# A two-layer kernel: layer 1's weights quantised during the experts, its products and recurrence turned to tokens on partitions

## The reference, cut to what matters

```python
u = rmsnorm(xn, norm_w)                       # per token
a = exp(-sigmoid(dt) * |A|)
x_t = a * x_(t-1) + sigmoid(dt) * (u @ Bmat)  # 64 states, over the 1024 tokens of a batch
s = x_t @ C + D                               # (tokens, 128)
def fp4(v):   # blocks of 16 along the last axis, scale = max|block| / 6, values on the grid 0..6
def lin(x, w): return fp4(x) @ fp4(w).T
f = lin(silu(lin(xn, w_gate)) * lin(xn, w_up), w_down)    # inner width 352
x = x + s * silu(f)
```

## Time and profile before

| what | us |
|---|---|
| timed runs, median of 3 | 1974.12 |
| timed runs, lowest and highest | 1966.82, 1975.07 |
| the profiled execution's own time | 1962.93 |
| its span, first to last instruction | 1960.8 |
| PE busy / DVE / ACT / POOL | 1828.6 / 1506.1 / 1012.8 / 1424.2 |
| mean granted TensorE clock | 0.971 |

### The profile page before, as it was taken

One profiled execution on the slowest core, in us unless ns is written; L12 is line 12 of the kernel. 1 busy time (PEld: TensorE's weight loads), 2 busy tenths in 40 slices (PEclk: granted clock), 3 DMA queues, 4 the chain that ended last, 5 costly groups with the idle time before them and its releaser, 6 DMA issues. The chain is left out here.

```text
span 1960.8 us, 33201 instructions
## 1 busy us (share of the span) xinstructions
PE 1828.6 (93%) x10425; PEld 1045.9 (53%) x10425; DVE 1506.1 (77%) x2045; ACT 1012.8 (52%) x1513; POOL 1424.2 (73%) x862
## 2 busy tenths in 40 slices
PE   6899999999999999999999999999998799965776
PEld 5455555555555555555555555555554688753345
DVE  5877777777777777777777777777777688787776
ACT  4345544454454455444544544554544588754543
POOL 3388888888888888888888888888887166636453
PEclk9899999999999999999999999999999799986899
DMA  6101010110101010101101010101010677230000
GB/s 219 45 12 55 19 54 21 43 46 19 54 11 54 11 55 19 54 21 43 45 21 54 11 54 11 55 19 54 21 43 21 216 246 243 79 92 19 0 17 27
DMA packets 98115, 107.82 MB, mean 55 GB/s; under 512 B 8224, under 2 KB 88032, under 8 KB 94880
## 3 DMA queue, kind: packets, MB, share of 16 engines
q1 hardware_dynamic: 93088, 97.15, 15.1%
q0 software_dynamic: 4992, 10.27, 1.5%
HBM read 52.56 MB, written 26.82 MB: 40 GB/s over the span
## 5 line engine op out<-in xcount | busy, mean ns | idle before, releaser
L1154 POOL TENSOR_TENSOR psum_k<-psum_k,probs 128x1024 f32<-128x1024 f32 x384 | 925.5, 2410 | 199.2 <-ACT probs L1099 184.2
L1171 DVE TENSOR_REDUCE mxh<-ps_m 128x2 f32<-128x1024 f32 x518 | 633.5, 1223 | 255.0 <-PE ps_m L931 253.4
L1099 ACT ACTIVATE probs<-ps_s 128x1024 f32<-128x1024 f32 x512 | 497.4, 1023 | 264.0 <-PE ps_s L948 212.8
L956 PE MATMUL ps_v<-probs,V 128*64 128x512 f32 x2056 | 489.8, 597 | 0.0
L1195 DVE RECIPROCAL rden<-den 128x128 f32<-128x128 f32 x260 | 245.6, 946 | 25.2 <-ACT den L1068 16.0
L956 PEld LDWEIGHTS ps_v<-probs,V 128*64 128x64 f32 x2056 | 137.2, 137 | 235.9 <-issue 233.4
L931 PE MATMUL ps_m<-k_hi,q_hi 64*128 64x512 f32 x1036 | 237.8, 452 | 11.1 <-DVE mxh L1171 7.2
L946 PE MATMUL ps_s<-q_lo,k_hi 64*128 64x512 f32 x1024 | 202.8, 389 | 0.0
L948 PE MATMUL ps_s<-shift,ones_r 64*128 64x512 f32 x1024 | 202.7, 388 | 0.0
L946 PE MATMUL ps_s<-q_hi,k_lo 64*128 64x512 f32 x1024 | 202.2, 389 | 0.0
L946 PE MATMUL ps_s<-q_hi,k_hi 64*128 64x512 f32 x1024 | 202.0, 390 | 0.0
(11 more groups left out here) (317 smaller groups left out, 2840.7 us busy)
## 6 DMA issues: line engine op xcount, KB each, us to landing
e_ew<-w_split SPq DMA_DIRECT2D x23, 1024.0 KB, 7.3
V<-V_next SPq DMA_DIRECT2D x33, 512.0 KB, 3.3
xs_hi<-xh SPq DMA_DIRECT2D x16, 512.0 KB, 3.7
xs_lo<-xl SPq DMA_DIRECT2D x16, 512.0 KB, 4.3
rows<-in_blank_d SPq DMA_DIRECT2D x4, 1483.5 KB, 18.6
e_x_raw<-rows SPq DMA_DIRECT2D x23, 258.0 KB, 3.5
we_raw<-in_experts_d SPq DMA_DIRECT2D x33, 128.0 KB, 2.4
w_split<-we_hi SPq DMA_DIRECT2D x32, 128.0 KB, 1.8
```

What stands on the lines that cost most here:

```text
L956: ins = nc.tensor.matmul(ps_v[rows, :], V[par][:, kt, rows], probs[:, t % RING, x, :], start=kt == 0, stop=kt == KT - 1)
L1099: nc.scalar.activation(probs[:, t % RING, :, :], ps_s[t % 2][:, :, :], ACT.Exp, scale=SCALE).then_inc(p_done, 1)
L1154: nc.gpsimd.tensor_tensor(acc, probs[:, (t - 1) % RING, :, :] if kt == 1 else acc, probs[:, t % RING, :, :], ALU.add).then_inc(add_done, 1)
L1171: nc.vector.tensor_reduce(mxh[:, kh, t, :], max_bank(unit, i)[:, :, :], AX.X, ALU.max).then_inc(m_done, 1)
```

## The change

In the experts:

- The shared weights are loaded after those of tiles 2 and 3, with layer 1's weights behind them; ACT splits the shared weights in tile 1 and DVE in tile 2.
- DVE runs steps 0 to 3 of the quantisation of layer 1's gate and up weights (128x768) and down weights (128x352) in blocks 9 to 12, ACT takes their sizes in tile 3, and POOL does the rest (four operations each, all in float32) ahead of its first scatter. They lie in the space of the `e_y` buffers, so `sums(0)` now also waits for PE's transposes of them, which stand in tiles 23 to 25.
- The transposes of the attention output go into the shared tiles 27 to 30 and the tail (`attended`), with ACT's silu four tiles after a chunk's own tile, and DVE's product (`gated`) behind it. The tail of PE has four `attended` ahead of the last `token_rows`; the tail of DVE has `gated(4)` between `weighted(5)` and `weighted(6)`, and so on.
- Half of X (batches 0 and 1) is loaded into the `y_row` buffers behind `sums(1)`.

In layer 1:

- No weights, no attention transposes and no X of batches 0 and 1 are loaded or formed at the start. The order is input, gate and up products, then states. Chunk 0 and chunk 1 are quantised one after the other, and `moments(3)` stands behind `hidden(0, 3)`.
- The down product has the transposed h stationary (12 products of 128 columns for three of 512), the recurrence the states stationary, with D added by a product of ones and a row (8 products of 128 columns). Both give tokens on partitions. `token_rows` and ACT's `finish` go; POOL adds x1 (`finish`) at the head of its stream for the chunk.
- One recurrence a chunk, behind its down product, in place of two groups of four.
- ACT takes the sizes of B and of the input ahead of `normalise`, `hidden_T` and `input_T` in chunks 0, 1 and 3.

The diff, cut to its core:

```diff
@@ expert_tiles, sync @@
-            sp.dma_start(ws_raw[:, :], g.inp["shared_d"]).then_inc(ws_in, 16)
             for s in range(2, NS):
                 rows(0, s)
                 weights(0, s)
+            sp.dma_start(ws_raw[:, :], g.inp["shared_d"]).then_inc(ws_in, 16)
+            for k, src in enumerate((g.inp["w_gate_d"], g.inp["w_up_d"])):
+                for j, (lo, n) in enumerate(IB):
+                    sp.dma_start(w_gu[0:n, 3 * k + j, :], src[lo:lo + n, :]).then_inc(w1_in, 16)
+            sp.dma_start(w_dn, g.inp["w_down_d"]).then_inc(w1_in, 16)
...
+            sp.wait_ge(w1T_ready, 3)
+            sums(0)
+            sums(1)
+            for v in range(4):
+                x = g.inp["X"][v // 2][v % 2 * CH:(v % 2 + 1) * CH, :]
+                sp.dma_start(y_row[v][:, :, :], x.rearrange("(n p) d -> p n d", p=P)).then_inc(g.x_early[v], 16)
+            for v in range(2, NCH):
                 sums(v)
@@ tensor @@
+                        if j == 2 and chunk_at(i, s, 0) in (0, 1, 2):
+                            layer1_weights(chunk_at(i, s, 0))
+                        if j == 1 and chunk_at(i, s, 4) is not None:
+                            attended(chunk_at(i, s, 4))
...
                 if q % FT == 0:
                     token_rows(*rows.pop(0))
+            for v in range(EARLY_A - 1, NCH):
+                attended(v)
             token_rows(*rows.pop(0))
@@ scalar @@
+                        if j == 3 and isinstance(i, int) and at(i, s) == 1:
+                            shared_high()
+                        if j == 2 and isinstance(i, int) and at(i, s) == 3:
+                            layer1_sizes()
+                        if j == 3 and chunk_at(i, s, 0) in (0, 1, 2):
+                            layer1_weights(chunk_at(i, s, 0))
+                        if j == 0 and chunk_at(i, s, 4) is not None:
+                            gate(chunk_at(i, s, 4))
@@ gpsimd @@
+            def scaled(k):
+                pool.wait_ge(w1_size, k + 1)
+                nc.gpsimd.tensor_scalar(m, m, 1.5, MAGIC, ALU.max, ALU.mult).then_inc(w1_grid, 1)
+                nc.gpsimd.tensor_tensor(val, val, m, ALU.add).then_inc(w1_grid, 1)
+                nc.gpsimd.tensor_tensor(val, val, m, ALU.subtract).then_inc(w1_grid, 1)
+                nc.gpsimd.tensor_tensor(val, val, w_s[k][:, :].unsqueeze(2).to_broadcast([P, nb, BLK]), ALU.mult).then_inc(w1_done, 1)
+            scaled(0)
+            scaled(1)
             with pool.Fori(0, ROUTED // NS) as i:
@@ vector @@
+                        if isinstance(i, int) and at(i, s) == 2 and j == 0:
+                            shared_low()
+                        if isinstance(i, int) and 0 <= at(i, s) * FT + j - 9 < 4:
+                            layer1_weights(at(i, s) * FT + j - 9)
+                        if j == 2 and chunk_at(i, s, 4) is not None:
+                            gated(chunk_at(i, s, 4))
...
-            for i, s in tail(3, NS):
+            for n, (i, s) in enumerate(tail(3, NS)):
                 weighted(i, s)
+                gated(NCH - 4 + n)
+            gated(NCH - 1)
@@ layer1, gpsimd @@
+            def finish(c):
+                pool.wait_ge(pr2_done, c + 1)
+                pool.wait_ge(stored, c * 16 + 1)
+                nc.gpsimd.tensor_tensor(out_t[:, :, :], pr2[:, :].rearrange("p (t d) -> p t d", d=D),
+                                        x1[:, c * TC:(c + 1) * TC, :], ALU.add).then_inc(o_done, 1)
             def body(c):
+                if not no_result(c):
+                    finish(c - 2)
@@ layer1, scalar, body @@
-                if c == 2:
-                    recurrence(0)
-                if c == 5:
-                    recurrence(1)
+                if c in (0, 1, 3):
+                    sizes_of_rest()
...
                 if not first(c):
                     gate(c - 1)
-                if not no_result(c):
-                    finish(c - 2)
+                    recurrence(c - 1)
@@ layer1, tensor @@
+            def recurrence(c):
+                for t in range(TC):
+                    nc.tensor.matmul(y, one[:, :], drow[:, :], start=True, stop=False)
+                    ins = nc.tensor.matmul(y, states[r, q // 2, tok], cmat[r, :], start=False, stop=True)
             def down(c):
                 pe.wait_ge(hT_done, c + 1)
-                for j, (lo, n) in enumerate(IB):
-                    ins = nc.tensor.matmul(ps_x, wT_dn[0:n, j, :], hqT[0:n, j, :], start=j == 0, stop=j == 2)
+                for t in range(TC):
+                    for j, (lo, n) in enumerate(IB):
+                        ins = nc.tensor.matmul(ps_x[:, tok], hqT[0:n, j, tok], wT_dn[0:n, j, :], start=j == 0, stop=j == 2)
...
             chunks(body)
-            pe.wait_ge(o_done, LAST - 1)
+            recurrence(LAST)
+            pe.wait_ge(y_done, NCH)
             last_hidden_T(0)
```

More of the change, by code:

```diff
@@ L281, in _, with layer1_early @@
             router(3)
+def layer1_early(nc, ctx, g):
+    sb, pb, sem = g.scope(ctx)
+    g.wT_gu = sb("wT_gu", [P, 2 * INNER], F32)
+    g.wT_dn = sb("wT_dn", [P, 3, D], F32)
+    g.y_row = [sb(f"e_y_row{s}", [P, CH // P, D], F32) for s in range(4)]
+    g.x_early = [sem(f"x_early{v}") for v in range(4)]
 def expert_tiles(nc, ctx, g):
@@ L558, in _ @@
                 high(i, q)
-            for i, s in tail(2, NS):
+            gate(NCH - 4)
+            for k, (i, s) in enumerate(tail(2, NS)):
                 result(i, s)
-            for v in range(NCH):
-                gate(v)
+                if k == 0:
+                    gate(NCH - 3)
+            gate(NCH - 2)
+            gate(NCH - 1)
         @block.gpsimd
@@ L627, in weighted, with shared_low, layer1_weights, gated @@
                         v.wait_ge(y_done, u + 2)
+            def shared_low():
+                v.wait_ge(wshi_done, 1)
+                nc.vector.tensor_tensor(ws[:, 2 * FF:4 * FF], ws_raw[:, :], ws[:, 0:2 * FF].bitcast(F32), ALU.subtract).then_inc(wslo_done, 1)
+            def layer1_weights(j):
+                for k in range(2):
+                    x = W1[k][0].rearrange("p (n k) -> p n k", k=BLK)
+                    if j:
+                        v.wait_ge(w1_step, 2 * j - 1 + k)
+                    else:
+                        v.wait_ge(w1_in, 7 * 16)
+                        v.wait_ge(w1_zero, 1)
+                    quantise_step(nc, j, x, w_s[k][:, :], w_rs[k][:, :], x, None).then_inc(w1_step, 1)
+            def gated(n):
+                v.wait_ge(gate_done, n + 1)
+                v.wait_ge(a_ready, n + 1)
+                part = g.gate[:, n * CH:(n + 1) * CH]
+                nc.vector.tensor_tensor(part, attended_at(n), part, ALU.mult).then_inc(a_done, 1)
             def body(i):
@@ L1418, in layer1 @@
     cmat = sb("cmat", [P, D], F32)
-    dcol = sb("dcol", [P, 1], F32)
+    drow = sb("drow", [1, D], F32)
+    one = sb("one", [1, P], F32)
     nw = sb("nw", [P, 1], F32)
@@ L1640, in _ @@
             chunks(body)
+            finish(LAST - 1)
         @block.scalar
@@ L1708, in gate @@
                 nc.scalar.activation(g1[:, :], ps_x, ACT.Silu).then_inc(g1_done, 1)
[L1710 to L1720 removed]
+            def recurrence(c):
+                act.wait_ge(y_ready, c + 1)
+                nc.scalar.activation(g.sT[:, c * CH:(c + 1) * CH], ps_h[c // LAST], ACT.Copy).then_inc(y_done, 1)
             def last_hidden_T(k):
@@ L1811, in _ @@
             v.sem_inc(stored, 1)
-            for k in range(2):
-                ins = nc.vector.memset(w_gu[IB[2][1]:P, 3 * k + 2, :], 0.0)
-            ins.then_inc(w_zero, 1)
             def decays():
```

307 lines of the change are left out of this document (146 added, 161 removed).

## The result

The changed kernel takes 1977.74 us (median of 14 runs, 1971.93 to 1984.02) where the kernel before takes 1971.67 on the same chip (14 runs): ratio 1.0033, interval 1.0021 to 1.0044. It is slower by about 6 us; 16 us faster was forecast. In two later comparisons, on chips where the kernel before takes 1964.69 and 1966.86 us, the same program came out at 1.0000 (0.9989 to 1.0012) and 1.0001 (0.9988 to 1.0014). They are called the second and the third chip here, that of the result the first (that it is another one is concluded from the 5 to 7 us between the medians of the kernel before). The kernel before has one profile only; its execution took 1962.93 us, less than any of the 14 timed ones, and on which chip it ran is not on record. So what is read from the first profile has to be split into what belongs to the kernel and what to the chip. The experiments do that.

What follows compares the result with a forecast made beforehand. PE was taken to bound the routed experts, DVE the shared tiles, and stream order the chunks, no engine being full. +10.4 - 11 - 14 - 1.5 = -16.1 us from 1962.93 gives 1946.8, plus 11.2 is 1958.0; range 1940 to 1975.

Steps and rivals of the forecast that it cites:

- the failed step: Layer 1's chunks, PE: a recurrence is 8 products of 0.22 us, 1.8 us, the same as `token_rows` took.
- C: Stretch of the seven chunks, to DVE's first reduction of chunk 7: forecast 14 us shorter.
- D: Stretch from DVE's first reduction of chunk 7 to the end of the span: forecast 1.5 us shorter.
- A: Stretch from PE's second group of token transposes to DVE's first weighted sum: forecast +4.9 us.
- B: Stretch from first weighted sum to chunk 0's first reduction: other expert terms +5.5 us, start of layer 1 -11.
- The second reason: Experts: POOL's scatters, begun late, run without pause, 23 x 6.04 us, ending at 1708.3 for 1703.4: +4.9 us.
- Shared tiles and end of the experts: Last expert tiles and tail: DVE's `gated` +3.2 us, a table load +0.5, queueing behind `attended(4)` +1.8.
- Rival D: Shared tiles: each of four silus between relus costs two table loads of 1.28 us, +4 us, 1962; chance 0.05.
- Start of layer 1: Before chunk 0: the DMA wait goes and chunk 0 is quantised alone, so it begins about 1793 for 1804: -11 us.
- Rival C: Chunks: one recurrence a chunk closes a ring through ACT's copy, 5.2 us each, +24 us in sum, 1998; chance 0.10.
- A, with the passes at 24.9 us: Rival at the start of the experts: POOL's quantising is dear, last scatter 12.9 us later still, 1971; chance 0.18.
- B's terms: Rival: experts hide all but 1 us at the first sum, chunks fall to PE's bound, -24; -31 us, 1943; chance 0.17.

Runs made afterwards that it cites:

- g3: The changed kernel with all products of the recurrence on 128 rows (zeros in the rest), on the third chip: ratio 0.9917 to the kernel before.
- c3: c1 with x added on VectorE behind its product instead of on GpSimd: ratio 0.9857 to the kernel before.
- c1: c2 with the recurrences of chunks 6 and 7 also moved to the start of the last chunk's PE work: ratio 0.9867 to the kernel before.
- c2: The changed kernel with the eight quantising passes on VectorE in tiles 20 to 22 and 128 rows in the recurrence: ratio 0.9868 to the kernel before.
- e5: Same program as g3, run earlier on another chip: the changed kernel with all recurrence products on 128 rows, ratio 0.9960 to the kernel before.

## Why the prediction was wrong

**The price of the recurrence: the failed step.** "`recurrence` is 8 of 0.22, 1.8" took the price of one product of `token_rows` with 128 rows for products of 1 and 64 rows in turn. With 1 and 64 rows in turn they take 0.415 us each at the full clock, 0.72 at half: 3.3 us a chunk, and 5.8 at half, for 1.8. It decides twice. In C, forecast 114 and measured 124.2 to 124.6, g3 has 119.1. In D, forecast 27.2 and measured 34.5, g3 has 25.7. g3's whole ratio, 0.9917, is the forecast's own (1958.0 to 1974.12, 0.9918), and this is partly luck: the other errors cancel there (A +2.1, B -5.3, C +5.1, D -1.5). The Trainium skill, "TensorE: Matmul & The Clock Gate", section "Step-by-step: what each phase is for", says that weight loads are pulled ahead of running matmuls when row groups don't conflict or the load goes to the background buffer, and that the row count K does not matter to a load. The trace agrees with the second (two loads of 1, 64 or 128 rows take 0.29, 0.29 and 0.30 us) and shows a place where the first gives nothing: in g3 each load starts 0.11 us ahead of its matmul, in the changed kernel the first load behind a change starts with it (1908.05 and 1908.06). Two rows of g3:

```profile
1921.77 0.30 PEld L2149 LDWEIGHTS ps_d<-cmat,states 128*128 128x128 f32 x2
...
1921.88 0.39 PE L2149 MATMUL ps_d<-cmat,states 128*128 128x128 f32 x2
```

**Experts: near where the chip has no ring, and only half for the reason given.** POOL's passes took 15.1 us for 12, and A grew by 5.7 and 7.5 us on two chips for +4.9. The delay by the wait for places is there. The second reason, that POOL then runs without a pause to the end, is not, and the prediction had named this as its sign. It carried the 6.04 us of the last groups of scatters through all 23; the early groups take 5.2 to 6.0 us on the third chip, so that POOL has caught up by its eleventh group and waits for ACT in each tile, as before the change:

```profile
1629.51 1.25 POOL L681 DMA_INDIRECT results<-e_y_row,e_y_at  x1 [1.15 <-ACT e_y_row L612]
```

That its last scatter ends 7.9 us later (1711.25 for 1703.4) comes from the tiles, which are late. What I left out is that POOL's passes lengthen DVE's operations beside them, to 2.3 us, in a tile that is 3.9 us longer. On the first chip A was +18.4. The prediction had the tiles late "by about 5 us" and stopped at DVE: it never asked who waits for the copy of places in turn, which is SyncE's rows and, behind them, the weights. Whether that chain makes the long tiles is not shown. They are the difference between 0.3% slower on the first chip and no difference on the others.

**Shared tiles and end of the experts.** Forecast +5.5; from the first weighted sum to the last `gated` 50.0 us for 45.9, +4.1. The wait of DVE for PE's `attended(4)` is there (3.80 us at 1769.49). Rival D fell: one table load at 1730.19, four in the program, relus behind a silu load nothing. The Trainium skill, "ScalarE: Activation LUTs", section "Table sets: the hidden batching unit", says that relu and copy are in every table set; this trace agrees.

**Start of layer 1.** Chunk 0 starts 34.7 us after the last `gated` of the experts; before, 49.5 us after their last silu: -14.8 us for -11. The first gate product comes after 19.8 us.

**Chunks beyond the recurrence.** With it mended they are 16.7, 19.8, 18.4, 22.8, 14.3, 14.1 and 13.0 us, against 17.6, 16, 21, 18, 14.5, 12 and 13, so 5 us are left in sum, with chunks 1 and 3 3.8 and 4.8 us over their forecast; there ACT's normalising, the inputs of the state and the silus stand ahead of what DVE waits for. Chunk 5 lost its stalls as forecast, 19.2 to 14.2 us in the changed kernel. Chunk 2 did not behave as said: in place of a wait of 5 us for sizes it has 3.65 us for ACT's copy of the recurrence and 3.06 for sizes. Rival C, a ring through ACT's copy of the recurrence, was the right place, at a far smaller price than its 26 us: DVE waits 7.4 us for that copy, up to 3.6, and chunk 4 takes 16.9 us, 14.3 with the recurrence mended. I priced C with the old wait and missed that the recurrence ahead of it doubles. POOL's `finish` costs DVE 0.8 us a chunk (5.6 us in seven), 0.4 forecast.

**The rivals' chances.** A, with the passes at 24.9 us, was wrong in price (15.1 us) and right in where it looked, but where the chip has no ring the recurrence cost more than POOL's place (14 us for 6 to 8). Within 0.5% had 0.18 and is what all three chips gave. Two sums of the prediction don't come out as written: B's terms give -30 us and 1944, not -31 and 1943, and nine tenths of 0.55, all of 0.17 and a small part of 0.18 make about 0.69 for faster, not 0.73.

## What to carry to other kernels

Price a matmul from a row of the same number of rows, and with the same neighbours. Where products of few and of many rows alternate on PE, try one number for all: zeros in the unused rows cost nothing and took 14 us off here. Ahead of a queue that returns buffers (scatters), put nothing that fits on another engine, and follow a late return to the end: who waits, what is queued behind it, and who waits for that. A program can pay for a late queue on one chip and not on the next, so time it beside its rivals on the same chip. The version c3 has the lowest ratio of all, 1.4% under the kernel before (1938.65 us for 1966.44); c1 and c2 lie within its interval.

## What was not expected of the hardware

A change between 1 and 64 rows from one product to the next costs 0.19 us (0.415 for 0.22), while 64 rows in a row cost what 128 cost (passes 0.11 us apart in both) and `down`'s changes between 128 and 96 rows cost nothing. GpSimd's max-and-multiply pass over 768 float32 columns took 3.31 us, its additions 2.08 and 2.14, and two VectorE operations beside them 2.3 instead of 0.69 us. The same program has tiles of 6.45 us on two chips and a ring of tiles up to 13.4 us on another, with the same order of instructions; with a second program (e5, which is g3) it was 16.0 us on one chip and no ring on another.
